# Sparse attention, cross attention and the quantized layer as one function on a grid of 19 steps per group

## What is computed

```
def _L3_attn_ref(query, key_param, Wq, bq, Wk, bk, Wv, bv, Wo, bo):    # 16 heads of 8, 32 keys
    queries = (query @ Wq + bq).reshape(B, L, H, E)
    keys_flat = k @ Wk + bk
    values = (keys_flat @ Wv + bv).reshape(B, S, H, D)
    A = sparsemax(scale * einsum(queries, keys))     # sort, cumulative sum, threshold, max(z - tau, 0)
    return einsum(A, values).reshape(B, L, H * D) @ Wo + bo
def _L3_xattn_ref(query, key, value, dropout_mask, Wout, bout, inv_scale_factor):
    probs = softmax(einsum('bqd,bkd->bqk', query, key) / 32) * dropout_mask
    return einsum('bqd,ed->bqe', probs @ value, Wout) + bout
def _L3_ffn_ref(x, weight_q, weight_scale, bias):
    x_scale = max(max|x|, EPS) / 127.0               # per token
    x_q = clip(round(x / x_scale), -128, 127)
    return (x_q @ weight_q.T) * x_scale * weight_scale + bias
x = x + _L3_attn_ref(_layernorm(x), ...)
x = x + _L3_xattn_ref(_layernorm(x), ctx_1024, ctx_1024, mask_BxSxS2_fk0, ...)
x = x + _L3_ffn_ref(_layernorm(x), ...)
```

## Time and profile before

| | us |
|---|---|
| median of 3 runs | 3303.65 (3302.57 to 3316.92) |
| the profiled execution, its own time | 3289.0 |
| span of the profile | 3287.2 |
| sparse attention, in the profile | 2700.0 to 3104.7 |
| cross attention | 3104.7 to 3205.0 |
| quantized layer with its last store | 3205.0 to 3287.2 |

### The profile page before, as it was taken

How to read it: one execution, slowest core, us unless ns; L and a number is a source line. 1 busy time by engine, 2 the same in 40 slices (tenths; PEclk the granted TensorE clock), 3 DMA queues, 4 the chain that set the end, 5 groups by cost and what they waited for, 6 DMA issues and landing times. The chain is left out here.

```text
span 3287.2 us, 53165 instructions
## 1 busy us (share of the span) xinstructions
PE 2502.1 (76%) x20491; PEld 1456.6 (44%) x20516; DVE 2093.7 (64%) x4141; ACT 1393.0 (42%) x2771; POOL 607.8 (18%) x581
## 2 busy tenths in 40 slices
PE   5777779999599799979979996788879924333361
PEld 3444446666344344435534444455545612222251
DVE  6888845555677455557754434687752228999657
ACT  4555537777332132223324432488723304434311
POOL 1333421111100033324410000111140030000003
PEclk8888879999799899979979997799979966667675
DMA  1000010000000000010000000200020110000010
GB/s 58 1 2 1 1 35 8 8 4 4 4 1 1 31 1 2 2 44 12 8 4 1 0 0 18 88 8 8 5 70 18 39 36 0 1 0 0 29 51 26
DMA packets 41988, 51.90 MB, mean 16 GB/s; under 512 B 9291, under 2 KB 30868, under 8 KB 40724
## 3 DMA queue, kind: packets, MB, share of 16 engines
q1 hardware_dynamic: 39700, 44.39, 4.3%
q0 software_dynamic: 2048, 4.20, 0.4%
HBM read 39.39 MB, written 9.18 MB: 15 GB/s over the span
## 5 line engine op out<-in xcount | busy, mean ns | idle before, releaser
L130 POOL TENSOR_TENSOR l_rstd<-l_moments,const_minus_half 128x4 f32<-128x4 f32 x104 | 118.9, 1143 | 1552.2 <-DVE l_moments L124 1525.8
L1422 PE MATMUL l_p_gate<-l_h_t,w_wg 128*128 128x512 f32 x400 | 208.9, 605 | 0.3 <-issue 0.2
L1445 PE MATMUL l_p_out<-l_hidden,w_wd 128*128 128x512 f32 x400 | 204.4, 594 | 3.7 <-DVE l_hidden L1715 2.4
L800 DVE TENSOR_REDUCE l_top<-l_ring 128x8 f32<-128x1024 f32 x128 | 150.9, 1221 | 79.5 <-PE l_ring L634 79.3
L2925 DVE SCALAR_TENSOR_TENSOR l_mix<-l_decay,l_cb 128x1024 f32<-128x1024 f32 x128 | 169.4, 1338 | 45.9 <-ACT l_decay L2808 43.5
L2808 ACT ACTIVATE l_decay<-l_p_ring 128x1024 f32<-128x1024 f32 x128 | 130.3, 1032 | 148.2 <-PE l_p_ring L2698 146.8
L348 ACT ACTIVATE l_probs<-l_probs,l_minus_top 128x128 f32<-128x128 f32 x512 | 156.7, 392 | 55.8 <-DVE l_minus_top L407 55.7
L1715 DVE TENSOR_TENSOR l_hidden<-l_act_out,l_p_spread 128x512 f32<-128x512 f32 x128 | 85.8, 686 | 128.9 <-ACT l_act_out L1543 128.7
L3185 PE MATMUL l_p_s<-const_ident,l_z 128*128 128x128 f32 x128 | 29.2, 421 | 179.5 <-ACT l_z L3224 179.5
L1205 DVE TENSOR_REDUCE l_minus_top<-l_p_score 128x4 f32<-128x1024 f32 x64 | 78.3, 1224 | 106.1 <-PE l_p_score L1033 102.5
L136 DVE TENSOR_SCALAR l_h<-x_res,l_moments,l_rstd 128x128 f32<-128x128 f32 (+1 forms) x384 | 112.6, 357 | 44.2 <-POOL l_rstd L130 43.9
(11 more groups left out here) (472 smaller groups left out, 6243.0 us busy)
## 6 DMA issues: line engine op xcount, KB each, us to landing
l_c_t<-in_ctx_t SPq DMA_DIRECT2D x24, 256.0 KB, 2.8
l_rows_in<-l_zero SPq DMA_DIRECT2D x1, 2432.0 KB
l_tile_h<-l_rows_in SPq DMA_DIRECT2D x38, 64.0 KB, 1.9
l_rows_out<-l_tile_y SPq DMA_DIRECT2D x38, 64.0 KB, 1.5
w_mask<-in_mask SPq DMA_DIRECT2D x1, 2048.0 KB, 9.2
w_wg<-in_l2f_wg SPq DMA_DIRECT2D x1, 2048.0 KB
w_wu<-in_l2f_wu SPq DMA_DIRECT2D x1, 2048.0 KB
w_wd<-in_l2f_wd SPq DMA_DIRECT2D x1, 2048.0 KB
```

Of the source, the lines that this page charges most:

```text
L130: return nc.gpsimd.tensor_tensor(rstd[:, :], moments[:, :, 1], minus_half[:, 0:moments.shape[1]], ALU.pow)
L800: nc.vector.tensor_reduce(top[:, b % 2, half * HALF:(half + 1) * HALF, 0], s, AX.X, ALU.max)\
L1422: nc.tensor.matmul(p_gate[k % 2][:, :], w["wg"][:, s, :], h_t[:, g % 4, :], start=True, stop=True)\
L1445: nc.tensor.matmul(p_out[:, :], w["wd"][:, s, :], hidden[:, k % 4, :], start=(s == 0), stop=(gated and s == steps - 1)).then_inc(down, 1)
```

## The change

The three layers become one function, `sparse_cross_quantized`, in the place of layer 9; layers 10 and 11 are gone, and their weights are fetched with those of layer 9. Time on each engine is cut into a list of steps g, with 19 to a group (PERIOD): the 15 sorting steps, the cumulative sum, the multiply, `tau` and the subtraction. Each part of each layer has a fixed offset from the step at which its group's sort begins: the sparse layer norm and scores at -15 to -9 (BEFORE), the chain behind `z` at 19 to 27 (BEHIND), the cross attention at 28 to 38 (IN_CROSS), the quantized layer at 39 to 47 (IN_QUANT). Every engine walks the same list and does, in each step, what falls due there. The order is fixed when the program is built, without loops. So while group i is sorted, the cross attention of group i - 1 is made at steps 9 to 18 (its addition at step 0 of the next), the quantized layer of group i - 2 at steps 1 to 8.

Other differences: the two additions at the end of the quantized layer move from POOL to DVE; each layer norm has its statistics two steps ahead of its application, with sorting steps between them; the two attentions and the quantized layer share the eight PSUM banks (`p_hq` takes the place of `p_misc` and `p_q`); the cross attention has one `probs` tile where it had two; SP stores each group as it is done and loads the tiles of the group three further on.

```
-def sparse_attention(nc, name, x, const, w, at):
+def sparse_cross_quantized(nc, name, x, const, w, at, aps):
...
+        SORTED = len(STEPS)
+        SCAN, INVERSE, TAU, SHIFT = SORTED, SORTED + 1, SORTED + 2, SORTED + 3
+        PERIOD = SHIFT + 1
+        BEFORE, BEHIND, IN_CROSS, IN_QUANT = -15, SHIFT + 1, SHIFT + 10, SHIFT + 21
+        FIRST, END = BEFORE, (NG - 1) * PERIOD + IN_QUANT + 8
...
+                for g in range(FIRST, END):
+                    if (k := group_at(g, BEHIND + 1)) is not None:
+                        transposes(k)
+                    for b in range(4):
+                        if (k := group_at(g, BEHIND + 2 + b // 2)) is not None:
+                            weigh(k, b)
+                    if (k := group_at(g, BEHIND + 5)) is not None:
+                        project(k)
+                    if (k := group_at(g, BEHIND + 7)) is not None:
+                        turn_out(k)
...
+                    if (k := group_at(g, IN_CROSS + 3)) is not None:
+                        cross_scores(k)
...
+                    if (k := group_at(g, IN_QUANT + 5)) is not None:
+                        turn_quant(k)
+                    if (k := group_at(g, IN_QUANT + 6)) is not None:
+                        product(k)
...
+                def quant_add(k):
+                    order.then(nc.vector.tensor_tensor(out8[:, :, :], out8[:, :, :], bcast(w["quant_bias"][:, :], [T, GROUP, D], 1),
+                                                       ALU.add))
+                    nc.vector.tensor_tensor(rows_of(k), rows_of(k), out8[:, :, :], ALU.add).then_inc(added, 1)
...
+                    if (k := group_at(g, IN_CROSS + 4)) is not None:
+                        cross_shift(k)
...
+                    if (k := group_at(g, IN_QUANT + 4)) is not None:
+                        largest(k)
+                    if (k := group_at(g, IN_QUANT + 5)) is not None:
+                        round_h(k)
+                    if (k := group_at(g, IN_QUANT + 7)) is not None:
+                        scale_output(k)
+                        quant_add(k)
...
-                def add_output(i):
-                    pool.wait_ge(scaled_columns, i + 1)
-                    nc.gpsimd.tensor_tensor(out[:, :, :], out[:, :, :], bcast(w["bias"][:, :], [T, GROUP, D], 1),
-                                            ALU.add).then_inc(biased, 1)
-                    pool.wait_ge(biased, i + 1)
-                    xs = x[:, bass.ts(i, GROUP), :]
-                    nc.gpsimd.tensor_tensor(xs, xs, out[:, :, :], ALU.add).then_inc(added, 1)
...
-ORDER = tuple(range(12))
+ORDER = tuple(range(10))
```

742 lines of the change are left out of this document (409 added, 333 removed).

## The result

| | before, in the same set | after |
|---|---|---|
| median of the runs | 3303.11 (4 runs) | 3263.56 (4 runs, 3262.05 to 3267.15) |
| ratio | | 0.9874, 95% interval 0.9845 to 0.9902 |
| the profiled execution, its span | 3289.0, 3287.2 | 3262.5, 3260.7 |
| the three layers in the profile | 587.2 | 542.9 |
| second set: median | 3285.44 (7 runs) | 3240.64 (4 runs), ratio 0.9863 (0.9847 to 0.9880) |

A set is a group of runs that were made together. The change makes the kernel 39.5 us faster in the first set and 44.8 in the second. Forecast were 3256 us and 47.9 us less; the range 3244 to 3280 holds the 3263.6.

The account below looks back on a forecast made before the run. DVE was taken as the bound, with 476.84 us of work in 587.2. Start 19.4, grid 462.2 and tail 57.7 sum to 539.3, 47.9 less, so the median 3303.65 becomes 3256 us; range 3244 to 3280 for 8 in 10.

Parts of the forecast that it names:

- Start: From the section's beginning to the first sort: nothing that anyone waits for is moved, so 19.4 us stay.
- POOL's waits: Sort's layer norm: 6.7 us of DVE waiting for POOL's power go, as two sorting steps now stand between.
- DVE pays 0 for the powers: Grid: POOL's powers beside sorting instructions cost DVE 0; each power itself is late by 0.9 us.
- rival A: Grid: by the shared port each of 20 powers delays a sorting instruction 0.86 us; +17, 3273 us; chance 0.11.
- Cross attention: Grid: 7.7 us of DVE per group, 52.5 us for seven groups, the last one's addition falling just behind the grid.
- quantized layer: Grid: 8.3 us of DVE per group with its two additions moved to DVE, 50.0 us for six groups.
- ACT's 6.3 us of waits go: Grid: DVE's 6.3 us of waiting for ACT's copies of unpaired elements vanish, covered by another group's normalization and rounding.
- Waits left in the grid: Scaling the product and shifting the scores: 0 to 2.7 us a period, 0.5 taken, 3.0 us in six full periods.
- Rival B: Grid: PE at the low clock, DVE waits 2.7 us in a full period; +15, 3271 us; chance 0.10.
- Rivals C and D: Whole kernel: hand-overs hidden only in part, 3288 us, chance 0.06; queues locking into each other, 3324 us, chance 0.03.
- The tail: Last subtraction to the end: 57.7 us, with the last group's cross attention and quantized layer running alone.
- The median: Whole kernel: the median's 14.7 us above the profiled execution carries over, so 3303.65 less 47.9 gives 3256 us.

Follow-up runs that it names:

- powers_five: Changed kernel with four more unread four-element powers on GpSimd behind each layer-norm power: 3263.4 us, one run.
- quant_behind: Changed kernel with the quantized layer's offset raised by seven periods, so behind the grid, and all loads ahead of the stores: 3323.4 us, one run.
- adds_on_pool: Changed kernel with the quantized layer's two additions back on GpSimd: 3262.3 us, ratio 0.9867 to the kernel before.
- warm_tensor: Changed kernel with two extra unread matmuls per group in PE's pause ahead of the 64 matmuls: 3240.5 us, ratio 0.9864 to the kernel before.
- grid_clock_alone: Changed kernel with four extra unread matmuls ahead of the 64 matmuls in every group but the last: 3237.9 us, ratio 0.9845 to the kernel before.

## Why the prediction was right, point by point

- **What bounds.** DVE as one stream: right. It is busy for 95% of the grid, and its work did not change by more than 1 us.
- **Start**, 19.4: measured 18.3 and 19.6.
- **POOL's waits**, 6.7 us gone: right. In the grid no wait for POOL is left, though a power takes up to 2.8 us where I had 1.9; the sorting steps between statistics and application cover it.
- **DVE pays 0 for the powers**, and rival A: decided for the forecast by powers_five. The section "Who interferes with whom" of the Trainium skill's page "SBUF — State Buffer" does not hold for a power of four elements beside a sorting instruction: neither 20 nor 100 of them lengthened one. Only GpSimd's side got longer there: the power took up to 2.8 us in place of 1.01. For additions of 512 elements it does hold in kind, where an instruction of 1.09 us took 2.18.
- **Cross attention** at 7.7 and **quantized layer** at 8.3 a group: 7.5 and 8.2 by quant_behind. The additions at 2 x 0.73 were no loss: on GpSimd they cost 1.1 of the 1.46 (adds_on_pool).
- **ACT's 6.3 us of waits go**: this step failed. The forecast said that the copy for step 7 now has the normalization and the rounding ahead of the step that needs it, which is true in a full period, and this term left out that the copy itself stands in ACT's list behind the projected copies and so behind the 64 matmuls. The paragraph on the waits that are left has that place, 2.0 us late if the matmuls take 7.7, and takes the row of 5.48 us, for which it names no late copy; they took 5.8 to 6.4 in six of eight groups. Measured are 12.5 us in place of 0. Only 3.5 of them lie in the five full periods. The other 9.1, in the first, second and last period, had no term in the forecast, which walked only full periods with the cover that they have.
- **Waits left in the grid**, 3.0 us, most of it at the product (step 8): mis-sized in the other direction. The product never waited in the grid, and the scores 1.1 us in all. PE was at the high clock once the 64 matmuls were over (turns of 0.66 us and queries of 1.11 behind them, where the lower level has 1.12 and 2.07). So of the grid's 6.1 us too many, the ACT copies bring 12.5, these places -1.9, the two layers' terms -2.0 (7 x 0.2 + 6 x 0.1); the other -2.5 us, by which the grid is shorter than these terms give, I can't place.
- **Rival B** (PE at the low clock) was the nearest to what happened, in its place and its mechanism, at 0.4 to 0.9 us in a full period in place of 2.7. Rivals C and D did not occur; no period is above 61.4 us, and from 64 on the forecast would have been wrong.
- **The tail**, 57.7: 56.3. To the last sparse addition 16.2 for 18.0, as PE's 16 turns took 2.64 us there and 3.67 in the kernel before; the cross attention alone 21.3 for 21.0, the quantized layer alone 12.8 for 12.8.
- **The median**: the section gave 44.3 us by the first profiles and the runs 39.5 and 44.8. That a median 14.7 us above the profiled execution carries over as a constant was luck more than insight; it came from 13 to 23 us by which the sets differ. The total was nearer than its terms deserved, too: in the grid 12.5 us of waits that were struck out stand against 6.4 by which other terms were too high.

## What to carry to other kernels

Put dependent, half-idle layers between the steps of the one that keeps its engine busy: their idle time goes and their work stays at the price of its rows, to within 0.2 us a group here. When several chains share the queues of the helping engines, look for each short operation that the bound engine needs at once, and see what stands ahead of it in its own engine's list: a copy of 1.0 us behind a result that takes 6 us to come costs more than its length, and one step in the order brought 5.8 us in the medians of one set (3240.6 to 3234.9). Look at the first and the last periods by themselves: they have less work to cover a late result. Whether a chain is slow can hang on the clock that TensorE was granted after a pause. Filling the pause ahead of a long batch can help, and the batch's duration tells whether the filling was enough; but the order is the first thing to mend, as two extra matmuls a group brought nothing here and four only 3.4 to 6.1 us of the section.

## What the runs showed of the hardware

- The 64 matmuls of 32 rows (128 records) took 3.85 us at the granted clock of 1.00 and 6.78 mostly at 0.50, and which of them came went with the pause ahead: 3.85 after pauses of 1.1, 2.2 and 2.5 us in warm_tensor, 6.0 to 6.8 after 3.7 and more. It is not the pause alone: grid_clock_alone has 5.48 after 1.9 us.
- A power of four elements on GpSimd takes 1.01 us alone and up to 2.8 beside VectorE's sorting instructions, and lengthens none of them (powers_five); an addition of 512 elements takes 1.26 alone, 2.0 to 2.1 beside them, and doubles one of them (1.09 to 2.18, adds_on_pool).
- In seven of fourteen traces VectorE stood for 10 to 25 us in all (the pauses of over 2.5 us) in the routed experts for no reason that the records show, and the others not at all.
- One and the same program's three last layers took 587.2, 587.2 and 592.1 us, and the copies' waits 6.3, 6.2 and 14.5. In the third the 64 matmuls took about 6.4 us in several groups, in the first at most 5.5.
